# A top-1 expert layer: token rows scattered into expert order, or token numbers sorted on chip and rows gathered, normed and scattered in each pass

## What is computed

```python
x_red = x @ w_red
logits = x_red @ wg_n.T
gates = softmax(logits, axis=1); scores = max(gates); idx = argmax(gates)
h = gelu(x @ W1[idx] + b1[idx])          # 256 -> 512
o = (h @ W2[idx] + b2[idx]) * scores     # 512 -> 256
x = layernorm(x + o)
```

## Time and profile before

| | |
|---|---|
| three runs | 2907.83 us median, 2907.33 to 2910.18 |
| the profiled execution | 2896.75 us, its span 2895.0 us |
| busy in the span | PE 2533.0 us (87%), DVE 1822.8, ACT 1576.4, POOL 1621.6 |
| first instruction of sort_by_expert | 1945.4 us |
| first instruction of expert_mlps | 2021.6 us |
| first instruction of add_experts | 2201.5 us |
| first instruction of layer1_self_attention | 2264.0 us |

### The profile page before, as it was taken

One profiled execution on the slowest core, in us unless ns is written; L12 is line 12 of the kernel. 1 busy time (PEld: TensorE's weight loads), 2 busy tenths in 40 slices (PEclk: granted clock), 3 DMA queues, 4 the chain that ended last, 5 costly groups with the idle time before them and its releaser, 6 DMA issues. The chain is left out here.

```text
span 2895.0 us, 43888 instructions
## 1 busy us (share of the span) xinstructions
PE 2533.0 (87%) x12067; PEld 1413.7 (49%) x12067; DVE 1822.8 (63%) x3044; ACT 1576.4 (54%) x2568; POOL 1621.6 (56%) x1344
## 2 busy tenths in 40 slices
PE   6999999999999999999999959971994688698595
PEld 4554555555555555555554434540673344454264
DVE  4776777777777777777777635662334565468743
ACT  4666676766667676666766625640222343454334
POOL 2777677777767777776777733424334213333343
PEclk8999999999999999999999979985997699899798
DMA  7454444555445455545544220003992100000242
GB/s 185 121 132 117 124 129 123 136 126 130 121 123 129 122 136 127 130 121 124 129 122 107 57 93 2 2 20 124 382 341 92 32 0 1 31 2 10 57 127 88
DMA packets 413442, 309.49 MB, mean 107 GB/s; under 512 B 296951, under 2 KB 341407, under 8 KB 408351
## 3 DMA queue, kind: packets, MB, share of 16 engines
q1 hardware_dynamic: 397118, 238.27, 31.8%
q0 software_dynamic: 12272, 63.92, 6.3%
q10 hardware_dynamic: 3952, 6.08, 0.6%
HBM read 193.33 MB, written 94.13 MB: 99 GB/s over the span
## 5 line engine op out<-in xcount | busy, mean ns | idle before, releaser
L760 POOL TENSOR_TENSOR a_total<-a_total,a_pr 128x1024 f32<-128x1024 f32 x384 | 915.5, 2384 | 268.9 <-ACT a_pr L745 251.1
L626 DVE TENSOR_REDUCE a_nmax<-a_psX 128x1 f32<-128x1024 f32 x512 | 623.8, 1218 | 279.8 <-PE a_psX L619 279.8
L745 ACT ACTIVATE a_pr<-a_psS 128x1024 f32<-128x1024 f32 x512 | 496.5, 1022 | 364.1 <-PE a_psS L732 344.1
L774 PE MATMUL a_psO<-a_pr,a_vd 128*64 128x512 f32 x2048 | 492.5, 602 | 0.0
L726 PE MATMUL a_psS<-a_qA,a_kA 128*128 128x512 f32 x1024 | 292.1, 406 | 8.3 <-DVE a_psS L680 4.4
L618 PE MATMUL a_psX<-a_kA,a_qA 64*128 64x512 f32 x512 | 232.8, 455 | 35.5 <-DVE a_nmax L626 31.3
L760 POOL TENSOR_TENSOR a_total<-a_pr 128x1024 f32<-128x1024 f32 x64 | 152.1, 2377 | 192.5 <-ACT a_pr L745 192.5
L774 PEld LDWEIGHTS a_psO<-a_pr,a_vd 128*64 128x64 f32 x2048 | 129.9, 136 | 241.6 <-issue 240.5
L696 DVE COPY a_psS<-a_least 128x1024 f32<-128x1024 f32 x192 | 232.6, 1212 | 4.6 <-ACT a_pr L745 4.6
L635 ACT ACTIVATE a_diag<-a_ident,a_nmax 128x128 fp32r<-128x128 f32 x512 | 186.0, 401 | 88.1 <-DVE a_nmax L626 88.1
L619 PE MATMUL a_psX<-a_kB,a_qA 64*128 64x512 f32 x512 | 232.8, 455 | 0.0
(11 more groups left out here) (423 smaller groups left out, 4881.1 us busy)
## 6 DMA issues: line engine op xcount, KB each, us to landing
a_qA<-a_qhi SPq DMA_DIRECT2D x248, 128.0 KB, 2.7
a_qB<-a_qlo SPq DMA_DIRECT2D x124, 256.0 KB, 3.8
a_vd<-a_vg SPq DMA_DIRECT2D x128, 128.0 KB, 2.3
a_kA<-a_khi SPq DMA_DIRECT2D x124, 128.0 KB, 2.6
a_kA<-a_klo SPq DMA_DIRECT2D x62, 256.0 KB, 3.6
a_qhi<-a_ph SPq DMA_DIRECT2D x120, 128.0 KB, 2.0
a_qlo<-a_pl SPq DMA_DIRECT2D x120, 128.0 KB, 2.1
a_khi<-a_ph SPq DMA_DIRECT2D x120, 128.0 KB, 2.0
```

Source lines behind the costliest of these rows:

```text
L626: w.eng.tensor_reduce(nmax[:, u:u + 1], psX[:, :, :].rearrange("p a k -> p (a k)"), AX.X, ALU.max, negate=True)\
L745: w.eng.activation(pr[:, n, :], both(psS[:, i % 2, :, :]), ACT.Exp, scale=SCALE).then_inc(sems["e"], 1)
L760: w.eng.tensor_tensor(total[:, buf, :], first, pr[:, n, :], ALU.add).then_inc(sems["ad"], 1)
L774: last = w.eng.matmul(psO[q * HD:(q + 1) * HD, :], vd[:, b, kc, :], pr[:, n, q * 512:(q + 1) * 512], start=p == 0 and i == 0, stop=p == KC ...
```

## The change

The expert layer is rebuilt in four parts. Line numbers of the changed kernel are its own.

1. **Sort.** No zero fill and no scatter. SP writes X as it is, in token order, to `rows_in` (four DMAs of 1 MB), then loads all weights of all 8 experts to SBUF: eight DMAs of 1 MB and two broadcasts of the biases (2 MB and 1 MB into SBUF). `pos` is taken apart into its slot (low 7 bits) and its tile. From these DVE makes zero-one tables: isL [128 tokens, 128 slots] and isH [128 tokens, 39 tiles] for each token tile. The table isH times the token number plus one (on POOL) and times the score (on DVE) stand side by side, and PE adds up over the 32 token tiles isL^T times that (fp32, 78 columns). So it gets, for each slot of each sorted tile, the token number and the score. Six short DVE steps make source rows, destination rows (an unused slot gets a spare row beyond the tokens) and scores.
2. **Expert pass.** POOL gathers the 128 tokens of a tile from `rows_in` (up to 7 tiles ahead). PE and DVE each read the tile's expert number from SBUF into a register and use it to address the weights and biases. b1 is added by DVE as it copies the hidden block, so ACT's GELU is one instruction of 512 columns. The score, the residual addition and the norm of a tile are done here, two tiles deep, and POOL scatters the finished rows to `rows_out` at their token numbers.
3. **Reload.** `add_experts` becomes `reload_tokens`: SP loads X back in token order, eight DMAs of 512 KB; PE transposes as before.
4. The hardware loop of the expert pass is gone (all 39 tiles are written out), and so are SP's loads and stores in it.

```diff
+class Experts(Room):
...
+    def loads(self, eng):
+        for e in range(self.W.shape[1]):
+            eng.dma_start(self.wt[:, e, :], self.W[:, e, :]).then_inc(self.loaded, 16)
+            if e == 0:
+                for tile, bias in ((self.b1s, self.b1), (self.b2s, self.b2)):
+                    eng.dma_start(tile[:, :, :].rearrange("p e h -> p (e h)"), bias.rearrange("e h -> (e h)").partition_broadcast(P))\
+                        .then_inc(self.loaded, 16)
...
@@ sort_by_expert, sync @@
-            for i in range(FILLS):
-                eng.dma_start(dst[:, i * n:(i + 1) * n, :], zero[:, :, :]).then_inc(sems["fill"], 16)
+            for i in range(PARTS):
+                eng.dma_start(dst[:, i * n:(i + 1) * n, :], X[:, i * n:(i + 1) * n, :]).then_inc(sems["xr"], 16)
+            mlps.loads(eng)
+            eng.wait_ge(sems["xr"], 16 * PARTS)
@@ sort_by_expert, gpsimd @@
-            for t in range(NT):
-                eng.indirect_dma_start(xs, bass.IndirectOffsetOnAxis(ap=pos[:, t:t + 1], axis=0), X[:, t, :], None)\
-                    .then_inc(sems["sc"], 16)
-            eng.wait_ge(sems["sc"], 16 * NT)
+            for i in range(PARTS):
+                g = quarter(i)
+                eng.wait_ge(sems["ih"], i + 1)
+                eng.tensor_tensor(val[:, g, 0, :], isH[:, g, :], token[:, g].unsqueeze(2).to_broadcast([P, NT // PARTS, NJ]), ALU.mult)\
+                    .then_inc(sems["vi"], 1)
@@ sort_by_expert, tensor @@
+            for t in range(NT):
+                if t % (NT // PARTS) == 0:
...
+                last = eng.matmul(psW[:, 0:2 * NJ], isL[:, t, :], val[:, t, :, :].rearrange("p v j -> p (v j)"), start=t == 0, stop=t == NT - 1)
@@ sort_by_expert, vector @@
-            eng.memset(zero[:, :, :], 0.0).then_inc(sems["z"], 1)
...
+            w.link(eng.tensor_scalar(lowi[:, :], pos[:, :], P - 1, None, ALU.bitwise_and), "dv")
+            w.link(eng.tensor_copy(low[:, :], lowi[:, :]), "dv")
+            w.link(eng.tensor_tensor(high[:, :], posf[:, :], low[:, :], ALU.subtract), "dv")
+            for i in range(PARTS):
+                g, n = quarter(i), NT // PARTS
+                eng.tensor_tensor(isH[:, g, :], high[:, g].unsqueeze(2).to_broadcast([P, n, NJ]),
+                                  slot_row.unsqueeze(1).to_broadcast([P, n, NJ]), ALU.is_equal).then_inc(sems["ih"], 1)
+                eng.tensor_tensor(isL[:, g, :], low[:, g].unsqueeze(2).to_broadcast([P, n, P]),
+                                  place.unsqueeze(1).to_broadcast([P, n, P]), ALU.is_equal).then_inc(sems["il"], 1)
+                w.wait("ih", i + 1)
+                eng.tensor_tensor(val[:, g, 1, :], isH[:, g, :], score[:, g].unsqueeze(2).to_broadcast([P, n, NJ]), ALU.mult)\
+                    .then_inc(sems["vs"], 1)
...
@@ expert_mlps @@
+        def up(w, j):
+            par = j % 2
+            if w.on("tensor") or w.on("vector"):
+                own[w.role, j] = w.eng.value_load(mlps.own[0:1, j:j + 1], min_val=0, max_val=wt.shape[1] - 1)
+            if w.on("tensor"):
+                if j == 0:
+                    w.eng.wait_ge(mlps.loaded, mlps.LOADS)
+                w.wait("xt", j + 1)
+                w.wait("uc", j - 1)
...
+            for j in range(SLOTS - 1):
+                gather(w, j)
...
+            for j in range(NJ + 3):
+                when(up, w, j + 2)
+                when(root, w, j - 1)
+                when(scatter, w, j - 3)
+                when(gather, w, j + SLOTS - 1)
+                when(turn_up, w, j + 1)
+                when(turn, w, j + 3)
+                when(down, w, j)
+                when(add, w, j)
+                when(shift, w, j - 1)
+                when(moments, w, j)
+                when(normed, w, j - 1)
...
-def add_experts(nc, X, xT, score, pos, os, hall):
+def reload_tokens(nc, X, xT, yrows, hall):
...
+            for j in range(NG):
+                eng.dma_start(X[:, j * GR:(j + 1) * GR, :], src[:, j * GR:(j + 1) * GR, :]).then_inc(sems[f"x{j}"], 16)
+            hall.loads(eng)
```

More of the change, by code:

```diff
@@ new lines, in turn_up, with down @@
+                w.wait("o", j - 1)
+                w.eng.activation(hT[:, par, :, :].rearrange("p a t -> p (a t)"), psH[:, par, :, :].rearrange("p a t -> p (a t)"), GELU)\
+                    .then_inc(sems["he"], 1)
+        def down(w, j):
+            par = j % 2
+            if w.on("tensor"):
+                w.wait("he", j + 1)
+                w.wait("od", j - 1)
+                for a in range(HC):
+                    last = w.eng.matmul(psO[:, par, 0:D], hT[:, par, a, :],
+                                        wt[:, bass.ds(own["tensor", j], 1), 2 * H + a * D:2 * H + (a + 1) * D], start=a == 0, stop=a == HC - 1)
@@ L2732, in walk @@
-        def walk(w):
-            for j in range(SLOTS):
-                load(w, j, j)
-            for j in range(SLOTS):
-                fetch(w, j, j)
-            for j in range(2):
-                turn(w, j)
-                load(w, SLOTS + j, j)
-            up(w, 0, 1)
-            up(w, 1)
-            turn(w, 2)
-            load(w, SLOTS + 2, 2)
-            turn_up(w, 0, 1)
-            for j in range(SLOTS):
-                tile(w, j, j, NJ - 1 - j)
-            trips = (NJ - 2 * SLOTS - 3) // SLOTS
-            w.loop(w.eng, trips, lambda i: [tile(w, SLOTS * i + SLOTS + k, k, NJ) for k in range(SLOTS)])
-            for j in range((1 + trips) * SLOTS, NJ):
-                tile(w, j, j % SLOTS, NJ - 1 - j)
-            if w.role == "sync":
-                for n in ("st0", "st1"):
-                    w.wait(n, w.at(n))
@@ new lines, in moments, with root @@
+        def moments(w, j):
+            if w.on("vector"):
+                w.wait("rd", j + 1)
+                w.eng.bn_stats(bst[:, j % 2, :], res[:, j % 2, :]).then_inc(sems["bn"], 1)
+        def root(w, j):
+            par = j % 2
+            if w.on("vector"):
+                w.wait("bn", j + 1)
+                w.eng.memset(idle[:, :], 0.0)
+                w.eng.bn_aggr(mv[:, par, :], bst[:, par, :]).then_inc(sems["var"], 1)
+            if w.on("gpsimd"):
+                w.wait("var", j + 1)
+                w.wait("y", j - 1)
+                w.link(w.eng.tensor_tensor(rs[:, par, 0:1], mv[:, par, 1:2], eps[:, :], ALU.add), "pl")
+                w.eng.tensor_tensor(rs[:, par, 1:2], rs[:, par, 0:1], mhalf[:, :], ALU.pow).then_inc(sems["rstd"], 1)
@@ new lines, in shift, with normed @@
+        def shift(w, j):
+            par = j % 2
+            if w.on("vector"):
+                w.wait("rstd", j + 1)
+                w.wait("y", j - 1)
+                w.eng.scalar_tensor_tensor(out=nb[:, par:par + 1], in0=mv[:, par, 0:1], scalar=-1.0, in1=rs[:, par, 1:2],
+                                           op0=ALU.mult, op1=ALU.mult).then_inc(sems["nb"], 1)
+        def normed(w, j):
+            par = j % 2
+            if w.on("scalar"):
+                w.wait("nb", j + 1)
+                w.wait(f"st{j % 4}", 16 * (j // 4))
+                w.eng.activation(yo[:, j % 4, :], res[:, par, :], ACT.Identity, bias=nb[:, par:par + 1], scale=rs[:, par, 1:2])\
+                    .then_inc(sems["y"], 1)
@@ new lines, in scatter, with when @@
+        def scatter(w, j):
+            if w.on("gpsimd"):
+                w.wait("y", j + 1)
+                w.eng.indirect_dma_start(yrows, bass.IndirectOffsetOnAxis(ap=mlps.dst[:, j:j + 1], axis=0), yo[:, j % 4, :], None)\
+                    .then_inc(sems[f"st{j % 4}"], 16)
+        def when(step, w, j):
+            if 0 <= j < NJ:
+                step(w, j)
+        def walk(w):
+            for j in range(SLOTS - 1):
+                gather(w, j)
+            turn(w, 0)
+            turn(w, 1)
+            up(w, 0)
+            turn(w, 2)
+            up(w, 1)
+            turn_up(w, 0)
+            for j in range(NJ + 3):
[10 more added lines that the diff above has]
+                when(normed, w, j - 1)
+            if w.role == "gpsimd":
+                for k in range(4):
+                    w.wait(f"st{k}", 16 * len(range(k, NJ, 4)))
@@ L2845, in normed @@
-        def normed(w, j):
-            q = j % 2
-            if w.on("scalar"):
-                w.wait("nb", j + 1)
-                for i in range(GR):
-                    w.eng.activation(X[:, j * GR + i, :], res[:, q, i, :], ACT.Identity, bias=nb[:, q, i:i + 1],
-                                     scale=rs[:, q, 1, i:i + 1]).then_inc(sems["y"], 1)
         def turn(w, j):
@@ L2901, in _ @@
             for j in range(NG):
[L2902 to L2909 removed]
+                turn(w, j)
         @block.scalar
```

340 lines of the change are left out of this document (131 added, 209 removed).

## The result

| | before | after |
|---|---|---|
| median, us | 2907.58 (2904.44 to 2910.18, 4 runs) | 2838.20 (2836.19 to 2841.84, 4 runs) |
| profiled execution: time, span | 2896.75, 2895.0 | 2837.65, 2835.9 |
| granted clock, mean | 0.937 | 0.948 |
| busy PE, DVE, ACT, POOL in after, us | | 2540.6, 1841.6, 1562.3, 1609.9 |

A forecast was written before the change was run, and what follows sets the result against it. PE bounds the expert pass, POOL's one-by-one indirect DMAs the sort's end and add_experts. Savings 30.6 + 3.3 + 3.0 - 4.0 + 45.0 - 0.5 = 77.4 us; 2907.8 - 77.4 = 2830, range 2818 to 2866.

The forecast's parts named there:

- The forecast case: Whole kernel: 2830 us, own range 2820 to 2840, chance 0.58.
- The quarter: Sort's end: one of four quarters of DVE's zero-one tables takes 2.25 us, all four 9.0.
- I take 1988.5: Sort's end: PE's table product ends at 1988.5, between 1987 and 1993.5; its 64 instructions 15.2 us cold, 7.4 warm.
- Start: Expert pass: first b2 addition at +16.2 us instead of 19.5, saving 3.3.
- Middle: Expert pass, first to last b2 addition: 153.5 us instead of 156.5, saving 3.0 if PE still sets the pace.
- The read at zero: Expert pass: the 39 expert-number loads each on PE and DVE are hidden and cost zero.
- the last one of part 2: Pass's end: last b2 addition to next stage takes 7.9 us instead of 3.9, losing 4.0.
- The 0.5 for the layer-1 loads: After the reload: layer-1 loads (1 MB) stand behind the reload's on SP, losing 0.5 us.
- VectorE as the pace: Rival, pass: DVE needs 4.5 or 4.7 us a tile, 14 to 21 us in all, 2844 to 2851; chance 0.20.
- PE stops at the load: Rival, pass: PE holds until its array has drained, 23 to 70 us in all, 2853 to 2900; chance 0.12.
- Late loads: Rival, pass's start: at 200 GB/s the loads end at 2017, `up` waits 20 us, 2850; chance 0.07.
- Slower than before: Rival, pass: uncovered load on PE at 2.4 us takes 94 us against 77, 2924; chance 0.03.

The follow-up runs named there:

- the warm products: 46 products without a reader run on TensorE before the table product, added to the changed kernel: 2828.31 us, ratio 0.9757; sort 44.82 us instead of 49.5.
- the moved drain: GpSimd's queue drained four more times within the pass, at tiles 8, 16, 24 and 32 of the changed kernel: 2830.2 us, ratio 0.9744.
- the earlier scatter: Changed kernel with each tile's scatter two steps behind instead of three, plus four extra drains and 46 products without a reader: 2822.73 us, ratio 0.9739.
- before's second profile: The kernel before, unedited, profiled once more: 2902.59 us, its pass 181.2 us where the first profile had 179.9.
- the run with seven a tile: Changed kernel with six more expert-number reads per tile on TensorE, one ahead of each product of up and down: 2901.45 us (one execution).

## Why the prediction was right, and where it was not

**The forecast case held**: 2838.2 in the range of 2818 to 2866, PE the pace of the pass, b2 additions 4.16 apart, no wait for weights, a reload under 20 us. Of the signs that it named, the sort's last step near 1990 (1991.7) came, the 8 us at the pass's end did not: 15.9. The median missed the forecast by 8 us, but the stretches missed it by 12, 4.0 at the sort's end and 8.0 at the pass's: with the warm products, the moved drain and the earlier scatter most of both came back. The 4 us between are what the medians gained more than the stretches did; no profile shows where, and that they made the total look better is luck.

**Sort's end, 30.6 forecast, 26.6 measured.** The four steps (0.88 for 0.85), the wide comparison (1.22 for 1.2) and the end after the product (2.5 for 2.5) fit. The quarter was 2.45 instead of 2.25, for the two engines' products beside each other. The step that failed is "I take 1988.5, since in the pass's ramp the clock came up once PE had begun to work without gaps": it did not come up. 64 instructions at 0.217 are 13.9 us (15.2 was my cold bound), and the run with the warm clock gives 15.33 for the whole, 4.6 less. I had the right bound in the text and chose from between on the strength of another product's ramp.

**Pass.** Start: 17.3 for 16.2; the first `up` came at 6.45 us for 5.4, on the gather's landing, and the rest followed. Middle: 153.8 for 153.5, but the 2.7 saved would be 3.9 against before's second profile. The read at zero was right. The Trainium skill's "DMA: Bandwidth & Descriptors", Latency and other measured facts, has a floor of about 600 ns for this read; the 390 reads of after and of the run with seven a tile took 294 to 565 ns, with medians of 299 to 318, so the measurement decides.

**Pass's end, lost 4.0 forecast, 12.0 measured.** The mis-sized term is the last one of part 2. It leaves out the drain, 6.4 us (shown by moving it: 5.6 back), and a scatter that waits for two others, 1.3 us (shown by the earlier scatter: 1.34 back). With both gone 8.9 are left, where the sum had 7.9; 0.7 of that is what remains of the drain. A drain was there to be read in before, 2.67 us at the end of the sort's 32 scatters.

**Reload, 45.0 forecast, 45.4 measured**, with PE's clock at 1.00 from 2189, 5 us after its first transpose, and the transfers at 351 to 361 GB/s. The 0.5 for the layer-1 loads can't be told from nothing: the stage took 479.6 and 478.1 us in before, 478.9 and 478.5 in after.

**The base.** The prediction subtracted from the runs' median and not from the profiled execution, and that was right: the profiled one was 11 us below the median, and its last stage took 151.4 us, 159.0 in the second profile.

**The rivals.** VectorE as the pace: out, a tile stays at 4.16. PE stops at the load: out for this placing, true between products. Late loads: out, and their cost when they are late is now known, 17 us. Slower than before: out; the run with seven reads a tile on PE, at 2901 (one execution), shows that reads between products can cost the whole gain.

## What to carry to other kernels

Indirect DMAs hidden under other work leave a bill: GpSimd's next drain took 0.08 us for each since the last one, so count them per stage, and drain where GpSimd has slack rather than before a meeting (here four drains cost the tiles 0.45 us in all, and a single one 3.9). Where TensorE has a short piece of work behind a long wait, price it at the clock that it had while waiting, unless a row of that same kind of work shows it rising. And before giving a second engine a share of elementwise work over the same tensor, look at what each takes alone: here a quarter of the tables took 2.45 us with the share and 2.32 without. And a stage that gets shorter by 4.6 us has not yet made the kernel faster by that: read the whole as well.

## What was not expected of the hardware

- A drain of GpSimd's queue took 0.05 us and 0.082 for each indirect DMA since the one before (0, 8, 9, 32 and 78 of them), with all of them landed.
- TensorE worked 13.49 of 14 us at clock 0.50 in the table product and stayed there; the same instructions, begun at 1.00, stayed at 1.00. In the reload, and in the products without a reader, the clock did rise from 0.50 to 1.00. Why it doesn't in the table product is open.
- VectorE's product of 312 columns took 0.98 us beside one on GpSimd over the same table, and 0.48 alone.
- A read of a number into a register of TensorE took 0.30 us; behind the eight instructions of `down` it was free, between products it cost 0.28.
